# One more stage split of a four-layer graph network: joint row statistics, two relus moved to VectorE, a message summed in one PSUM bank, and new instruction orders

## The chip, the cores and the metric

The kernel runs on one core of a Trainium2 chip. The metric is the device time of one execution in microseconds (us), as the median of three runs.

## The reference

The input `x` has 128 graphs of 128 nodes with 256 features; `adj` is one 128 x 128 adjacency for all graphs. Four residual layers follow each other, each on `h = relu(layernorm(x))`:

```
layer 0: hW = h W0;  e = leaky(hW a_self + (hW a_neigh)^T);  x += [softmax(e + mask) hW, hW]      (W0: 256 -> 128)
layer 1: x += deg * (h Wi^T + b) + adj (h Wj^T)
layer 2: 8-head masked attention on h, projected by Wo, plus biases;  x += ...
layer 3: Wh = h W3;  e = leaky(Wh a_src + (Wh a_dst)^T);  x += softmax(e, masked) Wh
```

`layernorm` subtracts the row's mean and divides by `sqrt(var + 1e-5)`; it has no weights.

## The kernel before, in words

The 128 graphs are worked in 64 groups of two (`GROUP = 2`). Everything of one group is cut into some 130 pieces, each a small function such as `stats0_0`, `norm0_1`, `rows_hi0`, `move0`, `feat0`. The digit behind the name is the layer. Each engine runs its own list of pieces, `slot`, once per step `t`; `at(part, piece)` says that in step `t` the piece works on group `t - part`. So each engine works on up to eight groups in one step, and a step is what one group costs the engine in all. The order within `slot` was written out by a search, and engines are tied together by semaphores alone (`wait_ge(piece_done, g + 1)`).

```
        def run(slot):
            for t in range(graph_groups + PARTS):

                def at(part, piece):
                    if 0 <= t - part < graph_groups:
                        piece(t - part)
                slot(at)
```

A layer begins with the statistics on VectorE (`bn_stats` for each of the two graphs, L718 to L884, then `bn_aggr`), a few very small operations on GpSimd that make `rstd` and `nshift` of them (L1170 to L1264), and the relu on ScalarE (L964, L973, L1006, L1012, L1023, L1026, L1087, L1091), one instruction of 256 columns for each graph. GpSimd splits the result in two f16 halves (`rows_hi`, `rows_lo`, L1185 to L1272), SyncE turns them with a DMA transpose (`move0` to `move3`), and TensorE multiplies each product in three f16 passes (`triple`, L403 to L405). Results leave PSUM by ScalarE (hi halves, exps, leaky relus) and VectorE (lo halves, maxima, updates of `x`). In layer 2 the attention result of each graph is normalised in PSUM on VectorE (L850, L859), its hi half made on ScalarE (L1080, L1084) and its lo half on VectorE (L864, L868). In layer 1 the node's own message and the gathered one are summed in two banks and added to `x` by two VectorE instructions (`update1_own` L781, `update1` L786).

All eight PSUM banks have several users, one behind the other in a step, named in the table `f0_ps = ps[3]` and so on.

Of the kernel before, what the change touches and what calls it, by code (L numbers as in the profile page):

```python
# [12 lines left out]
P = 128  # L13
D = 256
# [7 lines left out]
FOLD = [0, 1, 2, 5]  # L22
# [4 lines left out]
UNSCALE = 1.0 / WEIGHT_SCALE  # L27
Q_SCALE = UNSCALE * float(DH) ** -0.5
# [4 lines left out]
PARTS = 7  # L33
# [9 lines left out]
def build(nc, x_in, adj, adj_t, w0, w0_t, a0, w_i, w_j, b1, w_q, w_k, b_qk, w_v, b_v, w_o, b_o, w3, w3_t, a3, out):  # L43
# [7 lines left out]
    with ctx:  # L51
# [15 lines left out]
        deg_unscale = sb("deg_unscale", [P, 1], F32)  # L67
# [26 lines left out]
        stats0 = pair("stats0", [P, GROUP, 6], F32)  # L94
        moments0 = pair("moments0", [P, GROUP, 2], F32)
        vareps0, rstd0, nmean0, nshift0 = (pair(n, [P, GROUP], F32) for n in ("vareps0", "rstd0", "nmean0", "nshift0"))
        relu0 = pair("relu0", [P, GROUP, D], F32)
        stats1 = pair("stats1", [P, GROUP, 6], F32)
        moments1 = pair("moments1", [P, GROUP, 2], F32)
        vareps1, rstd1, nmean1, nshift1 = (pair(n, [P, GROUP], F32) for n in ("vareps1", "rstd1", "nmean1", "nshift1"))  # L100
        relu1 = pair("relu1", [P, GROUP, D], F32)
# [1231 lines left out]
```

## Time and profile before

| what | value |
| --- | --- |
| three runs | 1141.29, 1141.49, 1145.17 us, median 1141.49 |
| span of the profiled execution | 1144.0 us |
| its own time | 1145.17 us (the only run that is not shorter than the span) |
| TensorE busy | 1054.0 us, 92% |
| VectorE busy | 1043.0 us, 91% |
| ScalarE busy | 1056.3 us, 92% |
| GpSimd busy | 949.6 us, 83% |
| mean granted TensorE clock | 0.987 of 2.4 GHz |

The span runs from the first to the last instruction of one execution. The busy shares are averages over the filling of the pipeline, the steady part and its draining. Most ScalarE and VectorE instructions start before the one ahead has ended, so what an instruction costs is the distance from its start to the next start, and not the duration printed for it.

### The profile page before, as it was taken

To read this page: it belongs to the slowest core of one execution; us is meant where nothing else is said; L and a number is where in the kernel's file an instruction comes from. 1 tells how busy PE (TensorE), PEld (TensorE's weight loads), DVE (VectorE), ACT (ScalarE), POOL (GpSimd) and SP (SyncE) were. 2 spreads that over 40 slices of the span, in tenths; PEclk is the share of its full clock that TensorE was granted. 3 is DMA by queue.
4 is the path that set the end of the run, shared out by engine and by line. 5 is a ranking of instruction groups with operands and counts; after the bars stand their busy time and mean duration, and the time that the engine had idled before them with its cause. 6 is when DMAs were issued, how large, how long until landed. Compare 5 with 4: busy or idle time off the path is not lost.

```text
span 1144.0 us, 38802 instructions
## 1 busy us (share of the span) xinstructions
PE 1054.0 (92%) x14872; PEld 883.0 (77%) x14872; DVE 1043.0 (91%) x2911; ACT 1056.3 (92%) x3145; POOL 949.6 (83%) x1734
## 2 busy tenths in 40 slices
PE   4689999999999999999999999999999999999964
PEld 3467888788878878887887888888888888888752
DVE  4489999999999999999999999999999999999961
ACT  3489999999999999999999999999999999999862
POOL 3888899889989989988898988889888988998521
PEclk9899999999999999999999999999999999999997
DMA  5369999999999999999999999999999999999872
GB/s 149 68 110 167 180 177 182 167 187 171 181 176 178 171 169 182 180 179 168 182 167 179 183 178 173 169 189 171 174 176 183 170 168 190 180 174 156 151 139 51
DMA packets 643514, 190.05 MB, mean 166 GB/s; under 512 B 607232, under 2 KB 643328, under 8 KB 643328
## 3 DMA queue, kind: packets, MB, share of 16 engines
q1 hardware_dynamic: 642560, 187.24, 94.9%
q8 instruction: 117, 1.92, 0.7%
q14 instruction: 69, 0.57, 0.2%
q10 hardware_dynamic: 768, 0.33, 0.1%
HBM read 19.73 MB, written 16.78 MB: 32 GB/s over the span
## 4 chain that ended last, share of the span: by engine, by line
ACT 47%; DMA 16%; POOL 14%; PE 12%; DVE 9%; issue 3%; POOLq 0%; SPq 0%; DVEq 0%
DMA h_t<-h_rows 11%; PE ps L403 3%; DMA mix_t<-mix_rows 3%; PE ps L405 3%; PE ps L404 3%; ACT ps L1053 3%; ACT ps L1042 3%; ACT ps L1048 3%; ACT ps L1059 3%; POOL h_rows L1189 3%; POOL h_rows L1249 2%; ACT relu L973 2%; ACT relu L964 2%; ACT query_hi L1030 2%; ACT key_hi L1033 2%
## 5 line engine op out<-in xcount | busy, mean ns | idle before, releaser
L403 PE MATMUL ps<-w_hi,h_t 128*128 128x256 f16 (+2 forms) x1280 | 330.5, 265 | 31.4 <-DMA h_t<-h_rows 28.3
L404 PE MATMUL ps<-w_lo,h_t 128*128 128x256 f16 (+2 forms) x1280 | 329.5, 264 | 0.0
L405 PE MATMUL ps<-w_hi,h_t 128*128 128x256 f16 (+2 forms) x1280 | 326.4, 264 | 0.0
L403 PEld LDWEIGHTS ps<-w_hi,h_t 128*128 128x128 f16 x1280 | 125.3, 98 | 53.7 <-DMA h_t<-h_rows 33.0
L403 PE MATMUL ps<-h_t,w_hi 128*128 128x256 f16 x512 | 139.6, 273 | 0.0
L405 PE MATMUL ps<-h_t,w_lo 128*128 128x256 f16 x512 | 139.6, 273 | 0.0
L404 PE MATMUL ps<-h_t,w_hi 128*128 128x256 f16 x512 | 139.6, 273 | 0.0
L405 PEld LDWEIGHTS ps<-w_hi,h_t 128*128 128x128 f16 x1280 | 125.6, 98 | 14.3
L404 PEld LDWEIGHTS ps<-w_lo,h_t 128*128 128x128 f16 x1280 | 126.3, 99 | 13.2
L1185 POOL TENSOR_SCALAR h_rows<-relu 128x512 f16<-128x512 f32 x64 | 39.5, 618 | 64.3 <-ACT relu L964 64.3
L403 PEld LDWEIGHTS ps<-v_hi,head_t_hi 128*128 128x128 f16 x1024 | 79.9, 96 | 8.8 <-issue 2.3
L404 PEld LDWEIGHTS ps<-v_lo,head_t_hi 128*128 128x128 f16 x1024 | 78.7, 96 | 6.9 <-issue 0.3
L403 PE MATMUL ps<-v_hi,head_t_hi 128*128 128x33 f16 x1024 | 84.0, 178 | 0.0
L405 PE MATMUL ps<-v_hi,head_t_lo 128*128 128x33 f16 x1024 | 83.9, 177 | 0.0
L404 PE MATMUL ps<-v_lo,head_t_hi 128*128 128x33 f16 x1024 | 83.9, 177 | 0.0
L1048 ACT ACTIVATE ps<-ps,head_nmax 128x128 f32<-128x128 f32 x256 | 82.6, 527 | 0.0
L1221 POOL TENSOR_TENSOR x<-x,deg_b 128x512 f32<-128x512 f32 x64 | 81.6, 1275 | 0.0
L1241 POOL TENSOR_TENSOR x<-x,out_bias 128x512 f32<-128x512 f32 x64 | 81.3, 1270 | 0.0
L1053 ACT ACTIVATE ps<-ps,head_nmax 128x128 f32<-128x128 f32 x256 | 79.8, 484 | 0.0
L405 PEld LDWEIGHTS ps<-v_hi,head_t_lo 128*128 128x128 f16 x1024 | 78.6, 96 | 0.0
L1189 POOL TENSOR_TENSOR h_rows<-relu,h_rows 128x512 f16<-128x512 f32 x64 | 74.0, 1156 | 5.4
L1216 POOL TENSOR_TENSOR h_rows<-relu,h_rows 128x512 f16<-128x512 f32 x64 | 74.0, 1156 | 5.3
(181 smaller groups left out, 4622.4 us busy)
## 6 DMA issues: line engine op xcount, KB each, us to landing
x<-in_x SPq DMA_DIRECT2D x64, 256.0 KB, 3.9
out<-x SPq DMA_DIRECT2D x64, 256.0 KB, 2.7
h_t<-h_rows SPq DMA_TRANSPOSE x256, 3.6
head_t_hi<-head_hi SPq DMA_TRANSPOSE x64, 4.7
head_t_lo<-head_lo SPq DMA_TRANSPOSE x64, 6.2
mix_t<-mix_rows SPq DMA_TRANSPOSE x64, 3.4
w_f<-in_w_o SPq DMA_DIRECT2D x1, 256.0 KB, 4.1
w3t_f<-in_w_t SPq DMA_DIRECT2D x1, 256.0 KB, 3.8
```

The costliest lines, as they stand in the source:

```text
L403: pe.matmul(o, lh, rh, start=start, stop=False)
L404: pe.matmul(o, lh, rl, start=False, stop=False)
L405: return pe.matmul(o, ll, rh, start=False, stop=stop)
L1042: last = act.activation(sc0_ps[:, j * P:(j + 1) * P], sc0_ps[:, j * P:(j + 1) * P], ACT.Exp, bias=head_nmax[g % 2][:, 0, j:j + 1])
L1048: last = act.activation(sc1_ps[:, j * P:(j + 1) * P], sc1_ps[:, j * P:(j + 1) * P], ACT.Exp, bias=head_nmax[g % 2][:, 1, j:j + 1])
L1053: last = act.activation(sc2_ps[:, j * P:(j + 1) * P], sc2_ps[:, j * P:(j + 1) * P], ACT.Exp, bias=head_nmax[g % 2][:, 2, j:j + 1])
L1059: last = act.activation(sc3_ps[:, j * P:(j + 1) * P], sc3_ps[:, j * P:(j + 1) * P], ACT.Exp, bias=head_nmax[g % 2][:, 3, j:j + 1])
L1185: pool.tensor_scalar(h0_rows[g % 2][:, 0, :, :], relu0[g % 2][:, :, :], 1.0, 0.0, ALU.mult, ALU.add).then_inc(rows_hi0_done, 1)
L1189: pool.tensor_tensor(h0_rows[g % 2][:, 1, :, :], relu0[g % 2][:, :, :], h0_rows[g % 2][:, 0, :, :], ALU.subtract).then_inc(rows_lo0_done, 1)
L1216: pool.tensor_tensor(h1_rows[g % 2][:, 1, :, :], relu1[g % 2][:, :, :], h1_rows[g % 2][:, 0, :, :], ALU.subtract).then_inc(relu_lo1_done, 1)
L1221: pool.tensor_tensor(x[g % XBUF][:, :, :], x[g % XBUF][:, :, :], deg_b1[:, :].unsqueeze(1).to_broadcast([P, GROUP, D]), ALU.add)
L1241: pool.tensor_tensor(x[g % XBUF][:, :, :], x[g % XBUF][:, :, :], out_bias[:, :].unsqueeze(1).to_broadcast([P, GROUP, D]), ALU.add)
```

## The change

The change has six parts.

1. **Joint statistics.** One `bn_stats` reads both graphs of a group, element by element in turn, so that its even and odd results are those of the two graphs. The eight `bn_aggr` and half of the eight `bn_stats` of a step go. `add_eps` and `shift` move from GpSimd to VectorE, `negate_mean` goes.
2. **Outer relus on VectorE.** For layers 0 and 3, `relu(x - mean)` is one `tensor_scalar` from SBUF to SBUF for each graph on VectorE; the division by the deviation is put off to the copy of the features out of PSUM on ScalarE (`scale=rstd`). `keep_feat0` becomes two instructions.
3. **Message summed in one bank.** `agg` carries the weight scale, `gather` adds into the bank of `message_own`, and one VectorE instruction updates `x`.
4. **Heads split on GpSimd.** VectorE writes the normalised heads to `mix_f` in SBUF; GpSimd makes both halves of it for both graphs at once.
5. **Query and key bias on 64-row halves.** The four bias matmuls of a step read 64 rows each, query from the lower and key from the upper half, and come ahead of both products.
6. **New orders.** `PARTS` is 9 and no longer 7, all six orders and the bank table are new.

```diff
-PARTS = 7
+PARTS = 9
...
-            def stats0_0(g):
-                dve.wait_ge(x_moved[g % XBUF], 32 * (g // XBUF) + 16)
-                dve.bn_stats(stats0[g % 2][:, 0, :], x[g % XBUF][:, 0, :]).then_inc(stats0_0_done, 1)
...
-            def mean_var0(g):
-                dve.wait_ge(stats0_0_done, g + 1)
-                dve.bn_aggr(moments0[g % 2][:, 0, :], stats0[g % 2][:, 0, :])
-                dve.bn_aggr(moments0[g % 2][:, 1, :], stats0[g % 2][:, 1, :]).then_inc(mean_var0_done, 1)
+            def both_stats0(g):
                 dve.wait_ge(x_moved[g % XBUF], 32 * (g // XBUF) + 16)
+                dve.bn_stats(stats0[g % 2][:, :, :].rearrange("p b s -> p (b s)"), x[g % XBUF][:, :, :].rearrange("p b d -> p d b")).then_inc(both_stats0_done, 1)
+
+            def add_eps0(g):
+                dve.tensor_scalar(vareps0[g % 2][:, :], stats0[g % 2][:, :, 2], DEFER_VAR, DEFER_EPS, ALU.mult, ALU.add).then_inc(add_eps0_done, 1)
...
+            def norm0_0(g):
+                dve.tensor_scalar(relu0[g % 2][:, 0, :], x[g % XBUF][:, 0, :], stats0[g % 2][:, 0, 1:2], 0.0, ALU.subtract, ALU.max).then_inc(norm0_0_done, 1)
...
+            def shift1(g):
+                dve.wait_ge(power1_done, g + 1)
+                dve.scalar_tensor_tensor(nshift1[g % 2][:, :], stats1[g % 2][:, :, 1], -1.0, rstd1[g % 2][:, :], ALU.mult, ALU.mult).then_inc(shift1_done, 1)
...
-            def update1_own(g):
-                dve.wait_ge(message_own_done, g + 1)
...
             def update1(g):
+                dve.wait_ge(add_deg_bias_done, g + 1)
                 dve.wait_ge(gather_done, g + 1)
...
+                dve.scalar_tensor_tensor(x[g % XBUF][:, :, :], mi_ps[:, :].rearrange("p (b n) -> p b n", b=GROUP), degree_unscale[:, 0:1], x[g % XBUF][:, :, :], ALU.mult, ALU.add).then_inc(update1_done, 1)
...
-            def norm0_0(g):
-                act.activation(relu0[g % 2][:, 0, :], x[g % XBUF][:, 0, :], ACT.Relu, bias=nshift0[g % 2][:, 0:1], scale=rstd0[g % 2][:, 0:1]).then_inc(norm0_0_done, 1)
...
+            def keep_feat0_0(g):
+                act.activation(g0[g % 2][:, 0, 1:1 + F0W], f0_ps[:, 0 * F0W:1 * F0W], ACT.Copy, scale=rstd0[g % 2][:, 0:1]).then_inc(keep_feat0_0_done, 1)
...
-            def keep_out_0(g):
-                act.wait_ge(head_norm_0_done, g + 1)
...
+            def rows_hi_mix(g):
+                pool.wait_ge(head_norm_0_done, g + 1)
+                pool.tensor_scalar(mix_rows[g % 2][:, 0, :, :], mix_f[g % 2][:, :, :], 1.0, 0.0, ALU.mult, ALU.add).then_inc(rows_hi_mix_done, 1)
+
+            def rows_lo_mix(g):
+                pool.wait_ge(rows_hi_mix_done, g + 1)
+                pool.tensor_tensor(mix_rows[g % 2][:, 1, :, :], mix_f[g % 2][:, :, :], mix_rows[g % 2][:, 0, :, :], ALU.subtract).then_inc(rows_lo_mix_done, 1)
...
+                for e in range(KC):
+                    for bank, row, first in ((q_ps, 0, e), (k_ps, P // 2, KC + e)):
+                        pe.matmul(bank[:, e * GROUP * P:(e + 1) * GROUP * P], qk_bias[row:row + P // 2, first * P:(first + 1) * P], unit_rows[row:row + P // 2, 0:GROUP * P],
+                                         start=(e == 0), stop=False)
```

In the new bank table, `p0_ps`, `s0_ps`, `mi_ps` and `q_ps` are all `ps[7]`.

The order of VectorE in the middle of a step, around the statistics of layers 0 and 2. Before:

```order
L792 BN_STATS stats_0<-x 128x6 [waits update1_done]
L795 BN_STATS stats_0<-x 128x6
L830 TENSOR_TENSOR head_lo<-ps,head_hi 128x512 [waits keep_head_0_done]
L723 BN_STATS stats_1<-x 128x6 [waits x_moved_4]
L718 BN_STATS stats_1<-x 128x6 [waits x_moved_4]
L799 BN_AGGR moments_0<-stats_0 128x2 [waits stats2_1_done]
L800 BN_AGGR moments_0<-stats_0 128x2
L727 BN_AGGR moments_1<-stats_1 128x2 [waits stats0_0_done]
L728 BN_AGGR moments_1<-stats_1 128x2
```

Now:

```order
L716 BN_STATS stats_0<-x 128x6 [waits x_moved_10]
L786 BN_STATS stats_0<-x 128x6 [waits update1_done]
L880 RECIPROCAL inv_1<-sum_1 128x2 [waits expo3_1_done]
L719 TENSOR_SCALAR vareps_1<-stats_1 128x2
L729 TENSOR_SCALAR relu_0<-x,stats_0 128x256 [waits both_stats0_done]
L836 TENSOR_TENSOR head_lo<-ps,head_hi 128x512 [waits keep_head_3_done]
L790 TENSOR_SCALAR vareps_0<-stats_0 128x2 [waits both_stats2_done]
L725 TENSOR_SCALAR relu_0<-x,stats_0 128x256
L865 TENSOR_SCALAR vareps_0<-stats_0 128x2
```

The two pairs of statistics have become two single ones. Three `add_eps` (L719, L790, L865) and both relus of layer 0 (L729, L725), which read and write SBUF, stand between the work on PSUM.

The order of GpSimd in the new kernel, from the addition of layer 1's bias on:

```order
L1155 TENSOR_TENSOR x<-x,deg_b 128x512
L1134 TENSOR_TENSOR rstd_1<-vareps_1,minus_half 128x2 [waits add_eps0_done]
L1196 TENSOR_SCALAR h_rows<-relu_1 128x512 [waits norm3_0_done]
L1150 TENSOR_TENSOR rstd_0<-vareps_0,minus_half 128x2 [waits add_eps1_done]
L1138 TENSOR_SCALAR h_rows<-relu_0 128x512 [waits norm0_0_done]
L1200 TENSOR_TENSOR h_rows<-relu_1,h_rows 128x512 [waits rows_hi3_done]
L1184 TENSOR_SCALAR mix_rows<-mix_f 128x512 [waits head_norm_0_done]
L1159 TENSOR_SCALAR h_rows<-relu_0 128x512 [waits norm1_0_done]
L1188 TENSOR_TENSOR mix_rows<-mix_f,mix_rows 128x512 [waits rows_hi_mix_done]
L1163 TENSOR_TENSOR h_rows<-relu_0,h_rows 128x512 [waits rows_hi1_done]
L1172 TENSOR_TENSOR x<-x,out_bias 128x512
L1192 TENSOR_TENSOR rstd_1<-vareps_1,minus_half 128x2 [waits add_eps3_done]
```

The small operations are gone but for the four powers (two of them, L1134 and L1150, and L1192 here); the split of the heads (L1184, L1188) has joined. GpSimd now waits for VectorE at `rows_hi3`, the powers and `rows_hi_mix`.

## Rows read from the trace of the kernel before

**Rows 1.** 160 to 960 us: busy PE, PEld, DVE, ACT, POOL; clock, DMA share, GB/s
```profile
160.00:960.00 800.00, 775.03 (x11215) 656.15 (x11214) 774.57 (x2176) 789.04 (x2368) 714.86 (x1306) 1.00 1.03 176
```

**Rows 2.** VectorE's L718 (all, then from 118.5 us) and L895: ns min/median/max, first and last start
```profile
L718 DVE BATCH_NORM_STATS2 stats<-x x64: 405/410/423, 4.5 to 1029.2; 128x6 f32<-128x256 f32 x64
L718 DVE BATCH_NORM_STATS2 stats<-x x56: 408/410/423, 118.6 to 1029.2; 128x6 f32<-128x256 f32 x56
L895 DVE SCALAR_TENSOR_TENSOR x<-ps,inv,x x64: 471/477/481, 113.3 to 1140.7; 128x256 f32<-128x256 f32 x64
```

**Rows 3.** The chain that ended last, one turn: start us, us, what
```profile
551.11 0.60 ACT query_hi L1030
...
559.41 4.82 DMA h_t<-h_rows
...
565.22 0.11 PE ps L523
...
567.87 0.60 ACT query_hi L1030
```

**Rows 4.** The same chain on ScalarE, whose pieces run from start to start
```profile
502.99 0.49 ACT relu L973
...
512.79 0.28 ACT mix_rows L1084
...
516.11 0.26 ACT leaky L988
```

**Rows 5.** Timeline of VectorE in one step: start us, us, engine, line, operation
```profile
544.74 0.64 DVE L786 TENSOR_TENSOR x<-ps,x 128x512 f32<-128x512 f32 x1
...
546.67 0.42 DVE L868 TENSOR_TENSOR mix_rows<-ps,mix_rows 128x256 f16<-128x256 f32 x1
...
547.34 0.42 DVE L792 BATCH_NORM_STATS2 stats<-x 128x6 f32<-128x256 f32 x1
547.67 0.41 DVE L795 BATCH_NORM_STATS2 stats<-x 128x6 f32<-128x256 f32 x1
...
549.43 0.17 DVE L799 BATCH_NORM_AGGREGATE moments<-stats 128x2 f32<-128x6 f32 x1
549.51 0.15 DVE L800 BATCH_NORM_AGGREGATE moments<-stats 128x2 f32<-128x6 f32 x1
```

**Rows 6.** GpSimd's groups from 160 to 960 us: count | busy us, mean ns | idle before
```profile
L1221 POOL TENSOR_TENSOR x<-x,deg_b 128x512 f32<-128x512 f32 x48 | 60.9, 1269 | 0.0
...
L1189 POOL TENSOR_TENSOR h_rows<-relu,h_rows 128x512 f16<-128x512 f32 x48 | 55.5, 1156 | 4.0
...
L1201 POOL TENSOR_TENSOR rstd<-vareps,minus_half 128x2 f32<-128x2 f32 x49 | 34.0, 693 | 0.0
...
L1212 POOL TENSOR_SCALAR h_rows<-relu 128x512 f16<-128x512 f32 x48 | 29.7, 619 | 0.1
...
L1197 POOL TENSOR_SCALAR vareps<-moments 128x2 f32<-128x2 f32 x49 | 9.4, 191 | 4.1
```

**Rows 7.** Timeline of the start: start us, us, engine, line, operation
```profile
8.68 1.16 POOL L1189 TENSOR_TENSOR h_rows<-relu,h_rows 128x512 f16<-128x512 f32 x1
...
9.50 0.62 DVE L683 TENSOR_SCALAR qk_bias<-qk_bias_f 128x512 f16<-128x512 f32 x1
...
11.87 0.43 DVE L698 TENSOR_SCALAR mask<-adj_f 128x512 bf16<-128x512 f32 x1
...
12.85 0.35 DVE L704 TENSOR_SCALAR deg_b<-b_row,degree 128x256 f32<-128x256 f32 x1
...
41.05 1.16 POOL L1216 TENSOR_TENSOR h_rows<-relu,h_rows 128x512 f16<-128x512 f32 x1
41.22 1.53 DVE L713 SCALAR_TENSOR_TENSOR w_lo<-w_f,w_hi 128x516 f16<-128x516 f32 x1
42.16 1.72 POOL L1221 TENSOR_TENSOR x<-x,deg_b 128x512 f32<-128x512 f32 x1
```

**Rows 8.** L713, all seven: ns min/median/max, first and last start
```profile
L713 DVE SCALAR_TENSOR_TENSOR w_lo<-w_f,w_hi x7: 657/676/1534, 14.5 to 41.2; 128x512 f16<-128x512 f32 x6, 128x516 f16<-128x516 f32 x1
```

More of the change, by code:

```diff
@@ L394, in _ @@
         def _(pe):
-            def turn(bank, src, b):
-                for c in range(KC):
-                    last = pe.transpose(bank[:, (c * GROUP + b) * P:(c * GROUP + b + 1) * P], src[:, b, c * P:(c + 1) * P], ident[:, :])
-                return last
             def triple(o, lh, ll, rh, rl, start, stop):
@@ L580, in project_0, with project_1 @@
                     pe.wait_ge(w_split, W_TURN.index("o") + 1)
+                for c in range(KC):
+                    last = triple(pr_ps[:, 0 * D:1 * D], mix_t[g % 2][:, 0 * KC + c, :], mix_t[g % 2][:, (GROUP + 0) * KC + c, :], w_hi[:, c, COL_WO:COL_WO + D], w_lo[:, c, COL_WO:COL_WO + D],
+                                  start=(c == 0), stop=(c == KC - 1))
+                last.then_inc(project_0_done, 1)
+            def project_1(g):
+                if g == 0:
+                    pe.wait_ge(w_split, W_TURN.index("o") + 1)
                 pe.wait_ge(move_out_done[g % 2], 16 * (g // 2) + 16)
@@ L683, in bias_rows @@
                     made(dve.tensor_scalar(rows, full, WEIGHT_SCALE, None, ALU.mult))
[L684 to L688 removed]
+                    for row in (DH, P // 2 + DH):
+                        last = dve.scalar_tensor_tensor(rows[row:row + 1, :], full[row:row + 1, :], WEIGHT_SCALE, rows[row:row + 1, :], ALU.mult, ALU.subtract)
+                    last.then_inc(bias_ready, 1)
                 dve.wait_ge(bqk_turned, 1)
@@ new lines, in slot @@
+                at(3, update0_1)
+                at(6, head_max_2)
+                at(3, both_stats1)
+                at(3, add_eps1)
+                at(4, split_message)
+                at(6, head_max_0)
+                at(7, invert_heads_1)
+                at(3, shift1)
+                at(7, head_norm_1)
+                at(7, invert_heads_0)
+                at(7, head_norm_0)
+                at(4, update1)
+                at(6, head_max_1)
+                at(0, both_stats0)
+                at(4, both_stats2)
@@ new lines, in slot @@
+                at(9, inv_sum3)
+                at(1, add_eps0)
+                at(0, norm0_1)
+                at(6, split_head_3)
+                at(4, add_eps2)
+                at(0, norm0_0)
+                at(8, add_eps3)
+                at(6, split_head_2)
+                at(6, split_head_0)
+                at(6, split_head_1)
+                at(2, row_max0)
+                at(5, split_query)
+                at(9, update3_1)
+                at(9, update3_0)
+                at(4, shift2)
```

643 lines of the change are left out of this document (267 added, 376 removed).

## The prediction

> **What bounds the kernel now.** I read the busy time of the steady part first, then the starts of two VectorE lines, then the chain of waits.
>
> From 160 to 960 us ScalarE is busy 789.04 of 800 us (98.6%), TensorE 775.03 (96.9%), VectorE 774.57 (96.8%), GpSimd 714.86 (89.4%) [rows 1]. The reader is to see that no engine has room: the four are within 10% of each other.
>
> L718 runs once a step. From its start at 118.6 to that at 1029.2 us lie 55 steps, so a step takes 910.6 / 55 = 16.56 us [rows 2]. Times the shares, a step has 16.33 us of ScalarE, 16.04 of TensorE, 16.03 of VectorE and 14.80 of GpSimd.
>
> The chain says how ScalarE's step is stretched at times: from one `query_hi` at 551.11 to the next at 567.87 us it goes once round, 16.76 us, over ScalarE's layer-0 relus, GpSimd, a transpose of 4.82 us and the key and query products [rows 3]. So it is ScalarE, and beside it a loop through ScalarE of the same length.
>
> The whole span splits into 4.5 us before the first L718, 114.1 us for the first 8 steps (14.3 each), 910.6 for the 55 full ones, 111.5 from the last L718 to the last L895 (7.7 steps of 14.5 by L895's place at the end of part 7), and 3.3 behind it: 1144.0 us [rows 2].
>
> **The change, part by part, in us per step.** Prices are distances between starts.
>
> ScalarE: four relus of 0.49 and two `mix_rows` of 0.28 go, 2.52 in all; the split `keep_feat0` adds at most one instruction like the 0.26 one of 128 columns [rows 4]. 16.33 becomes 14.07. ScalarE stops being the bound, and the loop above loses its relus. What this can give is limited by the engine that is next.
>
> VectorE, removed: eight statistics at 0.33 (547.34 to 547.67), 2.64; eight aggregates at 0.08 or slightly less, 0.60; `update1` at 0.56 (0.64 less the overlap of 0.08); two lo halves of the heads, 0.67 (546.67 to 547.34) [rows 5]. Sum 4.47.
>
> VectorE, added: four joint statistics of 512 columns. No row has one. Two of the old, 0.66, is the upper bound, the 0.56 of a 512-column instruction the lower [rows 5]; I take 0.60, since the old ones are slightly dearer than the tensor operations of their width, so 2.40. Four `add_eps` and two `shift` at the aggregate's 0.07 to 0.08: 0.44. Four relus: L704 has this form, 256 columns with a scalar for each row, and takes 0.35 [rows 7], 0.26 from start to start; 0.33 would be the old statistics' pace. I take 1.04. Two instructions (`add_eps1`, `head_norm_0`) now stand directly behind what they wait for, 0.09 each, the part of an instruction that a following one hides (0.17 against 0.08) [rows 5]: 0.17. Sum 4.05. VectorE falls by 0.42 to 15.6.
>
> TensorE: four bias matmuls of 0.11 [rows 3] become two pairs. If the two halves of the array run side by side 0.22 goes, if not nothing: 15.8 to 16.0. `gather` and `message_own` cost as before.
>
> GpSimd: twelve small operations of 0.19 go, two of 0.62 and 1.16 come [rows 6]: 14.80 - 2.28 + 1.78 = 14.3, or 14.5 since small ones overlap their neighbours.
>
> DMA: the same transposes and loads, 176 GB/s at a share of 1.03 [rows 1]. Transfers wait for GpSimd in a new order, with a step more between producer and consumer. I cost that at nothing; what covers it is the added depth. If the cover fails, `make_query` behind `move2` is late, as it is now.
>
> Depth: VectorE's pieces span parts 0 to 9. Ten steps fill the pipeline instead of eight, and from the last statistics of layer 0 to the last update are 9.4 steps instead of 7.7. If the latency of one group sets their length, both stay at 114 and 112 us; if each step keeps its length they become 143 and 136. I take the middle, 128 and 124, since the new steps hold fewer pieces each but the engines are 85% full there. So time = 4.5 + 128 + 124 + 3.3 + 53 P = 260 + 53 P for a steady step P. The old span is met at P = 16.68.
>
> **The shared path of VectorE and GpSimd.** This decides. In the steady part before, each VectorE instruction has an operand in PSUM, or is a statistic, aggregate, reduction or reciprocal; GpSimd's durations hardly vary. At the start other kinds meet it. L713, two operands in SBUF, takes 0.68 alone [rows 8]. The one at 41.22 takes 1.53: GpSimd's L1216 ran until 42.21, and L713 ended 0.54 behind that. GpSimd's next, L1221 at 42.16, took 1.72 instead of 1.27. L683, a `tensor_scalar` from SBUF to SBUF, took 0.62 where L698 of the same width took 0.43; GpSimd was busy until 9.84, and L683 ended 0.28 later [rows 7]. So these kinds of VectorE instruction wait for the GpSimd instruction in flight to end, but for the first 0.13 us (0.68 - 0.54), and GpSimd waits for them in turn.
>
> The new kernel puts four `tensor_scalar` relus and two `shift` with two SBUF operands into each VectorE step. GpSimd's new step has five instructions of 1.16, two of 1.27, five of 0.62 and five of about 0.70 [rows 6]. An arrival at a random time waits, on average, the sum of (T - 0.13) squared over twice the step: (5 x 1.03² + 2 x 1.14² + 5 x 0.49² + 5 x 0.57²) / (2 x 17.2) = 10.7 / 34.4 = 0.31 us. In the new order one of the six, `norm3_0`, comes when GpSimd itself waits for it (`rows_hi3`). Five pay: 1.55. Bounds are 0, if all fall into GpSimd's pauses, and 5 x 1.0, if each meets the start of a long one. I take the mean because nothing in the order keeps those places free.
>
> P = 15.6 + 1.55 = 17.15 and the span is 260 + 909 = 1169 us. The profiled execution's own time of 1145.17 us is 1.2 above its span and 3.7 above the median of the runs; so 1169 stands for a median of 1167 us, 2% slower.
>
> The Trainium skill, SBUF — State Buffer, section "Who interferes with whom", has this rule: `copy`, `cast` and `tensor_scalar` in a two-port mode, and instructions with two SBUF inputs, share one pair of ports with GpSimd, and who comes second blocks until the first is done. The rows at 9.50 and 41.22 us agree. The rule reaches further than the rows, to the 2-column `add_eps`; that is the second rival.
>
> **Rivals.**
>
> *A, faster: the meetings cost little.* GpSimd has to wait for VectorE at `rows_hi3`, at the powers and at `rows_hi_mix`. If the steps settle so that the relus run in these pauses, VectorE needs 15.6 to 15.8, TensorE 15.8 to 16.0. With 0.3 us of friction, less than the 0.5 that VectorE idles now (3.2% of 16.56), P = 16.1 and the time 260 + 853 = 1113, median 1111. For it: both relus of layer 0 stand near the `add_eps3` for which `power3` waits. Against it: GpSimd works 14.5 of 16 us. It decides up to 1.08 us of waiting per step (16.68 - 15.6); beyond that the change loses.
>
> *B, slower still: the `add_eps` block too.* Ten instructions of a step then need the shared path. Three meet a waiting GpSimd (`norm3_0`, `add_eps1`, `add_eps3`), seven pay 0.31, and `norm0_1` directly behind `add_eps0` finds the GpSimd instruction that slipped in between, 0.77 instead of 0.31 (the mean instruction of 0.9 less 0.13). P = 15.6 + 2.17 + 0.46 = 18.2 and the time 260 + 965 = 1225, median 1222. No row shows a 2-column case of VectorE. In the Trainium skill, VectorE: DVE Perf Modes, section "Mode 2×_2P", a `tensor_scalar` takes both ports when the outermost dimension is even, which 2 is; by that rule B and not my sum would hold.
>
> *C, no gain: bank 7.* `p0`, `s0`, `mi` and `q` follow each other in one bank within one step, over all three of TensorE, ScalarE and VectorE. If each is late by a place in its queue, the loop takes a step of 16.6 to 17 and the time is 1140 to 1161. Against it: 12 matmuls of 0.11 [rows 3] here and 12 there, with copies of half a microsecond, fill only some 10 us of a step.
>
> **How the numbers follow.** About 0.5% (5.7 us) is what a measurement of this kernel can tell from no change. The forecast has 0.47, of which 0.05 lies within 0.5%, where waits come near 1.08. A has 0.35, all faster. B has 0.12, all slower. C has 0.06, of which 0.05 is within 0.5%. So faster 0.35, same 0.10, slower 0.55. The range from 1090 to 1245 runs from A without friction (P = 15.8: 1097) and a somewhat shorter filling to B with the fill and drain at their upper bound; some 0.05 is left out below and 0.1 above. The forecast's own range is 1145 (waits of 1.1) to 1200 (2.2).
>
> **What would show it.** ScalarE's steady share falls from 98.6% to about 82%, VectorE's stays above 95%. `both_stats` takes about 0.68, the relus 0.35 when free and up to 1.4 otherwise, in step with the end of a GpSimd instruction; GpSimd's own durations spread. The distance of `both_stats0` starts gives P. A P below 16.5 with relus at 0.35 throughout shows the sum wrong; `add_eps` above 0.15 in most steps shows B. Fill and drain are read from the first ten and last nine starts.

## The result, and the profile after

The changed kernel takes 1255.82 us in the median of four runs (1254.50 to 1257.21), the kernel before on the same chip 1143.33. The ratio is 1.0987, 95% interval 1.0964 to 1.1009. The forecast was 1167 us with a range of 1090 to 1245. The direction was right; the size was not, and the time lies outside the range.

The steady part by windows, of the changed kernel (busy PE, PEld, DVE, ACT, POOL; clock, DMA share, GB/s):

```profile
160.00:960.00 800.00, 723.56 (x10037) 570.43 (x10036) 795.09 (x1736) 651.84 (x1909) 632.36 (x739) 1.00 0.91 158
```

Beside [rows 1]: VectorE went from 96.8% to 99.4% of the stretch, and everything else fell: TensorE to 90.4%, ScalarE to 81.5%, GpSimd to 79.0%. The granted clock is 1.00 in both, so it has no part in this step. The chain that ended last, by engine and by line, says the same:

```profile
DVE 85%; issue 5%; PE 4%; DMA 2%; ACT 2%; SPq 1%; POOL 0%; POOLq 0%; DVEq 0%
DVE relu L729 6%; DVE vareps L719 5%; DVE x L780 4%; DVE stats L862 3%; DVE stats L759 3%; DVE mj_lo L775 3%; DVE head_lo L821 3%; DVE stats L716 3%; DVE x L858 3%; DVE head_nmax L810 3%; DVE stats L786 3%; DVE head_nmax L832 3%; DVE head_nmax L817 3%; DVE relu L868 3%; DVE key_lo L802 3%
```

At its head stand a relu of 256 columns (L729, `norm0_1`) and an instruction of two columns (L719, `add_eps0`), ahead of all work on 512 columns. The starts of single lines (ns min/median/max, first and last start; L716 is `both_stats0`, all and from its eleventh start; L719 `add_eps0`, L729 `norm0_1`, L725 `norm0_0`, L868 `norm3_0`, L883 `update3_0`):

```profile
L716 DVE BATCH_NORM_STATS2 stats<-x x64: 686/699/707, 4.0 to 1118.2; 128x6 f32<-128x512 f32 x64
...
L716 DVE BATCH_NORM_STATS2 stats<-x x54: 693/699/702, 141.7 to 1118.2; 128x6 f32<-128x512 f32 x54
...
L719 DVE TENSOR_SCALAR vareps<-stats x64: 145/1105/1106, 12.8 to 1137.3; 128x2 f32<-128x2 f32 x64
L729 DVE TENSOR_SCALAR relu<-x,stats x64: 340/1435/1441, 4.8 to 1120.5; 128x256 f32<-128x256 f32 x64
L725 DVE TENSOR_SCALAR relu<-x,stats x64: 340/341/1237, 5.0 to 1122.5; 128x256 f32<-128x256 f32 x64
L868 DVE TENSOR_SCALAR relu<-x,stats x64: 336/677/752, 99.4 to 1234.3; 128x256 f32<-128x256 f32 x64
L883 DVE SCALAR_TENSOR_TENSOR x<-ps,inv,x x64: 466/468/477, 131.0 to 1249.6; 128x256 f32<-128x256 f32 x64
```

From 141.7 to 1118.2 us lie 53 steps: P = 976.5 / 53 = 18.42 us, where the forecast had 17.15. The span is 4.0 + 137.7 + 976.5 + 131.4 + 3.2 = 1252.8 us. The medians of L719 and L729 lie at their maxima: these two are late in nearly every step, and by the same amount. L725, the same instruction as L729 for the other graph, is not.

Timeline of VectorE and then of GpSimd over the same stretch of one steady step (start us, us, engine, line, operation):

```profile
598.42 0.29 DVE L765 TENSOR_SCALAR vareps<-stats,message_var,message_eps 128x2 f32<-128x2 f32 x1
598.62 0.74 DVE L775 SCALAR_TENSOR_TENSOR mj_lo<-ps,message_unscale,mj_hi 128x512 f16<-128x512 f32 x1
599.28 0.68 DVE L810 TENSOR_REDUCE head_nmax<-ps 128x4 f32<-128x512 f32 x1
...
603.49 0.15 DVE L880 RECIPROCAL inv<-sum 128x2 f32<-128x2 f32 x1
603.56 1.11 DVE L719 TENSOR_SCALAR vareps<-stats 128x2 f32<-128x2 f32 x1
604.58 1.44 DVE L729 TENSOR_SCALAR relu<-x,stats 128x256 f32<-128x256 f32 x1
605.93 0.68 DVE L836 TENSOR_TENSOR head_lo<-ps,head_hi 128x512 f16<-128x512 f32 x1
606.53 0.15 DVE L790 TENSOR_SCALAR vareps<-stats 128x2 f32<-128x2 f32 x1
606.60 0.34 DVE L725 TENSOR_SCALAR relu<-x,stats 128x256 f32<-128x256 f32 x1
606.86 0.15 DVE L865 TENSOR_SCALAR vareps<-stats 128x2 f32<-128x2 f32 x1
```

```profile
598.80 0.69 POOL L1150 TENSOR_TENSOR rstd<-vareps,minus_half 128x2 f32<-128x2 f32 x1 [0.99 <-DVE vareps L765]
...
602.36 1.16 POOL L1188 TENSOR_TENSOR mix_rows<-mix_f,mix_rows 128x512 f16<-128x512 f32 x1
603.48 1.16 POOL L1163 TENSOR_TENSOR h_rows<-relu,h_rows 128x512 f16<-128x512 f32 x1
604.59 1.27 POOL L1172 TENSOR_TENSOR x<-x,out_bias 128x512 f32<-128x512 f32 x1
607.10 0.70 POOL L1192 TENSOR_TENSOR rstd<-vareps,minus_half 128x2 f32<-128x2 f32 x1 [1.24 <-DVE vareps L865]
```

`add_eps0` starts 0.08 us after GpSimd's L1163 and ends at 604.67, 0.03 after L1163's end at 604.64. `norm0_1` starts 0.01 ahead of the start of L1172 and ends at 606.02, 0.16 after L1172's end at 605.86. From 605.86 to 607.10 GpSimd waits for `add_eps3` (L865), and all that VectorE does there on SBUF is free. So the two engines wait for each other in turn, both within 4 us. On the shared path itself only VectorE pays: GpSimd's instructions keep their length beside it (ns min/median/max from 160 to 960 us), though the forecast expected them to spread.

```profile
L1163 POOL TENSOR_TENSOR h_rows<-relu,h_rows x44: 1153/1156/1162, 161.3 to 953.6; 128x512 f16<-128x512 f32 x44
L1172 POOL TENSOR_TENSOR x<-x,out_bias x44: 1262/1268/1269, 162.4 to 954.7; 128x512 f32<-128x512 f32 x44
```

From start to start `add_eps0` takes 1.02 us where 0.07 is its free price (606.53 to 606.60 for L790), `norm0_1` 1.35 where 0.26 is (606.60 to 606.86 for L725). With `norm3_0` (mean 0.60) and `norm3_1` (0.38) the waits are 0.95 + 1.10 + 0.34 + 0.11 = 2.50 us per step. The other six of the ten pay nothing.

### The profile page after: what moved, and what is told of

It is laid out like the page before. It is cut to its first block, busy times and chain, and to the rows that moved or that the text cites. A ratio compares the mean times of both kernels' runs of the same rounds, so it can differ in the third digit from the quotient of the medians.

```text
span 1252.8 us, 37773 instructions
## 1 busy us (share of the span) xinstructions
PE 1089.4 (87%) x14872; PEld 855.1 (68%) x14872; DVE 1184.8 (95%) x2600; ACT 969.7 (77%) x2825; POOL 933.2 (74%) x1094
## 4 chain that ended last, share of the span: by engine, by line
DVE 85%; issue 5%; PE 4%; DMA 2%; ACT 2%; SPq 1%; POOL 0%; POOLq 0%; DVEq 0%
DVE relu L729 6%; DVE vareps L719 5%; DVE x L780 4%; DVE stats L862 3%; DVE stats L759 3%; DVE mj_lo L775 3%; DVE head_lo L821 3%; DVE stats L716 3%; DVE x L858 3%; DVE head_nmax L810 3%; DVE stats L786 3%; DVE head_nmax L832 3%; DVE head_nmax L817 3%; DVE relu L868 3%; DVE key_lo L802 3%
## 5 line engine op out<-in xcount | busy, mean ns | idle before, releaser
L978 ACT ACTIVATE prob<-leaky,nmax 128x128 f32<-128x128 f32 x64 | 25.8, 402 | 126.4 <-DVE nmax L735 126.4
L618 PE MATMUL ps<-g,prob_t 128*128 128x256 f32 x256 | 72.1, 405 | 31.9 <-DVE head_lo L836 31.0
L386 PE MATMUL ps<-v_hi,head_t_hi 128*128 128x33 f16 x1024 | 90.8, 178 | 9.8 <-DMA head_t_lo<-head_lo 3.5
L1150 POOL TENSOR_TENSOR rstd<-vareps,minus_half 128x2 f32<-128x2 f32 x64 | 44.9, 702 | 68.7 <-DVE vareps L765 68.7
L1192 POOL TENSOR_TENSOR rstd<-vareps,minus_half 128x2 f32<-128x2 f32 x64 | 44.9, 702 | 68.5 <-DVE vareps L865 68.5
L388 PE MATMUL ps<-v_hi,head_t_lo 128*128 128x33 f16 x1024 | 90.1, 177 | 0.0
L387 PE MATMUL ps<-v_lo,head_t_hi 128*128 128x33 f16 x1024 | 90.0, 178 | 0.0
L729 DVE TENSOR_SCALAR relu<-x,stats 128x256 f32<-128x256 f32 x64 | 85.6, 1337 | 0.0
L393 PE MATMUL ps<-ident,g 128*128 128x128 f32 x256 | 51.1, 282 | 39.2 <-DVE key_lo L802 31.4
L1155 POOL TENSOR_TENSOR x<-x,deg_b 128x512 f32<-128x512 f32 x64 | 84.2, 1315 | 0.0
L1172 POOL TENSOR_TENSOR x<-x,out_bias 128x512 f32<-128x512 f32 x64 | 81.2, 1269 | 0.0
```

The source lines that it names most:

```text
L386: pe.matmul(o, lh, rh, start=start, stop=False)
L387: pe.matmul(o, lh, rl, start=False, stop=False)
L388: return pe.matmul(o, ll, rh, start=False, stop=stop)
L393: pe.matmul(bank[:, b * P:(b + 1) * P], feats[:, b, col:col + 1].to_broadcast([P, P]), ident[:, :], start=(b == 0), stop=False, is_transpo ...
L618: last = pe.matmul(s3_ps[:, b * D:(b + 1) * D], prob_t3[g % 2][:, b * P:(b + 1) * P], g3[g % 2][:, b, 0:D], start=True, stop=True)
L729: dve.tensor_scalar(relu0[g % 2][:, 1, :], x[g % XBUF][:, 1, :], stats0[g % 2][:, 1, 1:2], 0.0, ALU.subtract, ALU.max)
```

## The experiments

Each kernel is compared with the kernel before on its own chip; steps are the mean distance of starts in the middle of the run, from the 21st start of layer 0's statistics to the 50th.

**1. The five moved behind row_max0.** The block L719, L729, L790, L725, L865 stands where GpSimd waits:

```diff
-                at(1, add_eps0)
-                at(0, norm0_1)
...
                 at(6, split_head_1)
                 at(2, row_max0)
+                at(1, add_eps0)
+                at(0, norm0_1)
+                at(4, add_eps2)
+                at(0, norm0_0)
+                at(8, add_eps3)
                 at(5, split_query)
```

> Edit: in VectorE's order of the changed kernel, add_eps0, norm0_1, add_eps2, norm0_0 and add_eps3 move as one block behind row_max0; nothing else. Theory S (waits on the path that VectorE shares with GpSimd): in the changed kernel add_eps0 and norm0_1 lose 0.95 and 1.10 us per step to the GpSimd instructions in flight; behind row_max0 GpSimd has finished add_out_bias and itself waits for add_eps3, so both run at 0.07 and 0.26 and the step falls from 18.42 to about 16.4 us, the span to 1115 to 1145. Rival L (VectorE's own load and the longer pipeline make the loss): the work is the same, so the step stays at 18.4 and the span at 1253.

1183.45 us, ratio 1.036 (1.0324 to 1.0396): 72 us come back without one instruction less. The step is 17.11. All five are free, but another waits now, `shift2` (L794); its line, and the place beside GpSimd's `add_feat0` (L1146):

```profile
L794 DVE SCALAR_TENSOR_TENSOR nshift<-stats,rstd x64: 160/623/637, 49.5 to 1120.1; 128x2 f32<-128x2 f32 x64
...
609.96 0.68 POOL L1146 TENSOR_TENSOR x<-x,g 128x256 f32<-128x256 f32 x1
610.03 0.63 DVE L794 SCALAR_TENSOR_TENSOR nshift<-stats,rstd 128x2 f32<-128x2 f32 x1
```

In the changed kernel it took 0.144 in the median. GpSimd finishes `power2`, for which `shift2` waits, and goes straight on to L1146; `shift2` comes 0.07 us too late. It costs 0.48 for the lock, and 0.2 more of the wait for `power2` ahead of it. So the step came to 17.11 and not 16.4.

**2. One column in place of two**, in `add_eps0` alone.

```diff
-                dve.tensor_scalar(vareps0[g % 2][:, :], stats0[g % 2][:, :, 2], DEFER_VAR, DEFER_EPS, ALU.mult, ALU.add).then_inc(add_eps0_done, 1)
+                dve.tensor_scalar(vareps0[g % 2][:, 0:1], stats0[g % 2][:, 0, 2:3], DEFER_VAR, DEFER_EPS, ALU.mult, ALU.add)
+                dve.tensor_scalar(vareps0[g % 2][:, 1:2], stats0[g % 2][:, 1, 2:3], DEFER_VAR, DEFER_EPS, ALU.mult, ALU.add).then_inc(add_eps0_done, 1)
```

> Edit: add_eps0 as two instructions of one column each instead of one of two columns, in the same place. Theory S with the rule that a tensor_scalar takes the shared ports only if its outermost dimension is even: both run at once, norm0_1 then meets the GpSimd instruction before (0.8 us) and add_eps2 the next one (0.4), so 2.05 becomes about 1.2 and the step about 17.6, the span about 1210. Theory S without that rule: one column blocks as well, step 18.4 or a little more. Rival L: 18.4 to 18.5, one small instruction more.

1214.67 us, ratio 1.0633 (1.0597 to 1.067), step 17.67. The first of the two single columns, in the run with them:

```profile
L719 DVE TENSOR_SCALAR vareps<-stats x64: 126/132/143, 12.7 to 1096.4; 128x1 f32<-128x1 f32 x64
...
602.15 1.16 POOL L1164 TENSOR_TENSOR h_rows<-relu,h_rows 128x512 f16<-128x512 f32 x1
...
602.34 1.12 DVE L730 TENSOR_SCALAR relu<-x,stats 128x256 f32<-128x256 f32 x1
```

In 64 cases the first never took over 0.143 us and the second (L720) never over 0.152, at the very place in the order where the two-column form took 1.105. The relu behind them (L730 here) now meets the same GpSimd instruction by itself and takes 1.12. So two columns take the shared path and one does not. In the Trainium skill, VectorE: DVE Perf Modes, section "Mode 2×_2P", the outermost dimension of more than one element must be even, or odd and equal on both sides, for `tensor_scalar` to use both ports; a single column has no such dimension, and both runs agree.

**3. The relus back on ScalarE**, the rest as changed. The bias is the negated mean, by one two-column reduction on VectorE for each layer:

```diff
-                dve.tensor_scalar(relu0[g % 2][:, 1, :], x[g % XBUF][:, 1, :], stats0[g % 2][:, 1, 1:2], 0.0, ALU.subtract, ALU.max)
+                dve.tensor_reduce(nmean0[g % 2][:, :], stats0[g % 2][:, :, 1:2], AX.X, ALU.max, negate=True).then_inc(negate_mean0_done, 1)
...
+                act.activation(relu0[g % 2][:, 1, :], x[g % XBUF][:, 1, :], ACT.Relu, bias=nmean0[g % 2][:, 1:2])
```

> Edit: the four outer relus of a step go back to ScalarE (relu of x minus the mean, still with the deviation put off), VectorE makes the negated means with one tensor_reduce per layer. Theory S: norm0_1 and norm3 lose 1.55 us of waits with 1.05 us of work; VectorE needs 15.0 plus up to 1.0 for add_eps0, ScalarE 15.0 + 1.96 = at most 17.0, so the step is 16.1 to 17.0 and the span 1130 to 1180. Rival L, with load alone: VectorE loses 1.05 us only, step 17.3, span about 1195.

1204.04 us, ratio 1.0538 (1.0502 to 1.0574), step 17.36: better, but a miss. The number is that of the rival, which counted VectorE's load alone (17.3), but the reason is another. `shift1`, `add_eps2` and `shift2`, all free in the changed kernel, wait here:

```profile
L768 DVE SCALAR_TENSOR_TENSOR nshift<-stats,rstd x64: 111/561/1115, 34.1 to 1112.0; 128x2 f32<-128x2 f32 x64
L789 DVE TENSOR_SCALAR vareps<-stats x64: 153/478/1119, 50.5 to 1132.4; 128x2 f32<-128x2 f32 x64
L793 DVE SCALAR_TENSOR_TENSOR nshift<-stats,rstd x64: 141/812/821, 51.4 to 1136.3; 128x2 f32<-128x2 f32 x64
```

Together these waits are 1.3 us per step, and VectorE idles 0.7 more for GpSimd's `power1`. Taking work away moves the meetings and does not end them.

**4. The kernel before with its outer relus on VectorE**, the rest as before, each pair directly behind its `mean_var`:

```diff
                 at(0, mean_var0)
+                at(0, norm0_1)
+                at(0, norm0_0)
...
                 at(6, mean_var3)
+                at(6, norm3_1)
+                at(6, norm3_0)
```

> Edit on the kernel before: the four outer relus alone move to VectorE (with the deviation put off to the copies of the features), behind the aggregates of their layer; seven parts, old order otherwise. Theory S: VectorE has 16.03 + 1.04 = 17.1 us of work and 0.3 to 0.6 us of waiting for each relu, 1.2 to 2.4 in all: step 18.3 to 19.5, span 1240 to 1305. Without a shared path: step 17.1, span about 1175. If the relus cost nothing where ScalarE is the bound: 1144 or less.

1194.83 us, ratio 1.048 (1.0429 to 1.0532), step 17.27. I had expected waits and there were none, a miss; the two relus of layer 3 on VectorE:

```profile
L897 DVE TENSOR_SCALAR relu<-x,moments x64: 352/353/355, 96.4 to 1171.5; 128x256 f32<-128x256 f32 x64
L900 DVE TENSOR_SCALAR relu<-x,moments x64: 345/348/350, 96.6 to 1171.8; 128x256 f32<-128x256 f32 x64
```

They stand directly behind the aggregate for which GpSimd's `add_eps3` waits. The relus of layer 0 are free too, 0.353 and 0.348 in the median. The loss here is VectorE's load alone: before, it was busy for 16.03 us of a step, and 4 x 0.265 more is 17.09; it is busy for 17.14 of 17.27. Moving these relus is wrong for this kernel even without the shared path.

**5. Joint statistics alone**, and **6.** with layer 3's relus on VectorE, and **8.** with both layers':

```diff
-                dve.bn_stats(stats0[g % 2][:, 0, :], x[g % XBUF][:, 0, :]).then_inc(stats0_0_done, 1)
...
+                dve.bn_stats(stats0[g % 2][:, :, :].rearrange("p b s -> p (b s)"), x[g % XBUF][:, :, :].rearrange("p b d -> p d b")).then_inc(mean_var0_done, 1)
```

> The kernel before with part 1 of the change alone: one joint bn_stats per layer, no bn_aggr; add_eps, negate_mean and shift stay on GpSimd, all relus on ScalarE. A joint statistic costs 0.60 to 0.62 us from start to start in the changed kernel, two old ones 0.66 and two aggregates 0.15, so VectorE loses 8 x 0.33 + 0.60 - 4 x 0.61 = 0.80 us of its 16.16 us of work per step. Theory L (each engine's own load): ScalarE keeps 16.36 us and stays the bound, so the step stays at 16.5 to 16.6 and the time between 1134 and 1143 us, ratio 0.993 to 1.0. Rival T (the four engines are tied so closely that any load taken from one shortens the step): step 16.2, about 1120 us.

1138.35 us, ratio 0.9964 (0.9947 to 0.9982), the only kernel of the study below the kernel before, and hardly. Its steady part:

```profile
160.00:960.00 800.00, 780.85 (x11298) 663.10 (x11287) 765.58 (x1612) 794.65 (x2391) 723.15 (x1315) 1.00 1.04 178
```

ScalarE is busy 99.3% where it was 98.6% [rows 1]: the bound was elsewhere. The instructions that went were dearer by 0.8 us than those that came, VectorE's busy time fell by 0.33 (16.03 to 15.70), and 0.15 of a step was bought.

> The kernel before with joint statistics and with the relus of layer 3 alone on VectorE (the deviation goes into the copy of the features; negate_mean3 and shift3 go from GpSimd). Theory L: ScalarE falls by two relus of 0.49 to 15.4 us, VectorE goes from 16.16 to 16.16 - 0.80 + 0.53 = 15.9, TensorE keeps 16.07. The step is then TensorE's and VectorE's, 16.1 to 16.3, and the time 1115 to 1130 us. Both relus stood at 0.27 from start to start, without a wait, when both layers were moved (0.262 and 0.269). Rival S (VectorE waits for GpSimd here too, now that the loads are closer): relus up to 0.6 each, step 16.6 and more, no gain over the kernel before.

1186.42 us, ratio 1.0379 (1.0356 to 1.0401): a clear miss. `norm3_1` is L854 here; its line, and its place beside `rows_lo0` (L1148):

```profile
L854 DVE TENSOR_SCALAR relu<-x,stats x64: 342/1169/1215, 90.3 to 1163.2; 128x256 f32<-128x256 f32 x64
...
607.38 1.22 DVE L854 TENSOR_SCALAR relu<-x,stats 128x256 f32<-128x256 f32 x1
```

```profile
607.28 1.16 POOL L1148 TENSOR_TENSOR h_rows<-relu,h_rows 128x512 f16<-128x512 f32 x1
```

The relu that was free in run 4 waits here 0.7 us on average and is late in nearly every step, since GpSimd is at L1148 when it comes. That this is so because layer 0's work stayed with ScalarE is likely, but no run shows it. These 0.7 us are most of the 0.9 by which the step of 17.15 missed the forecast's upper end.

> e4_before_relus_on_vector with joint statistics: the kernel before with both outer layers' relus on VectorE and no aggregates. That run had a step of 17.27 with VectorE never idle and no relu waiting, so VectorE's load alone set it. Theory L: 17.27 - 0.80 = 16.47, time 1191.3 - 53 x 0.80 = 1149 us, some 0.5% above the kernel before; more than with one layer moved. Rival S: with GpSimd's pauses (2.3 us per step there) shrinking, the relus begin to wait, step 17 and 1175 us.

1157.67 us, ratio 1.0142 (1.0119 to 1.0165), step 16.61. Two relus more on VectorE than in run 6, and 29 us less: here they are all free again (0.26 to 0.29 from start to start), as the sum of the loads said.

**7. The changed kernel with every wait mended.** The block of five stands as in run 1; beside it:

```diff
-                dve.scalar_tensor_tensor(nshift2[g % 2][:, :], stats2[g % 2][:, :, 1], -1.0, rstd2[g % 2][:, :], ALU.mult, ALU.mult).then_inc(shift2_done, 1)
+                dve.tensor_scalar(nshift2[g % 2][:, 0:1], stats2[g % 2][:, 0, 1:2], rstd2[g % 2][:, 0:1], -1.0, ALU.mult, ALU.mult)
+                dve.tensor_scalar(nshift2[g % 2][:, 1:2], stats2[g % 2][:, 1, 1:2], rstd2[g % 2][:, 1:2], -1.0, ALU.mult, ALU.mult).then_inc(shift2_done, 1)
...
-                at(8, norm3_0)
...
                 at(6, head_max_2)
+                at(8, norm3_1)
+                at(8, norm3_0)
                 at(3, both_stats1)
...
-                at(7, norm3_1)
...
+                at(4, power1)
                 at(9, rows_hi3)
-                at(4, power1)
```

> The changed kernel with the group of five moved behind row_max0 as in e1_group_later, and two places more mended: norm3_1 and norm3_0 stand directly ahead of both_stats1, with rows_hi3 on GpSimd behind power1, so that GpSimd waits for add_eps1 while they run; and shift2 is two one-column instructions with a pointer, which e2_one_column found free of the wait. Nothing of the computation is changed. e1_group_later had a step of 17.11, of which 0.48 was shift2's wait, 0.34 and 0.11 those of the norm3 pair. Theory S (the waits are the loss): step 17.11 - 0.93 + 0.10 = 16.28, first ten steps and drain as there (136, 130), span 7 + 266 + 53 x 16.28 = 1136 us. Rival M (GpSimd's lost time only comes up elsewhere): one of the other arrivals is blocked in its turn, or GpSimd becomes late, and the step stays above 16.8, over 1163 us.

1170.27 us, ratio 1.0238 (1.0213 to 1.0264): 85 us below the changed kernel. `norm0_1` (L729) and `norm3_0` (L869 here), and what VectorE waited for from 160 to 960 us (us in total, times, longest):

```profile
L729 DVE TENSOR_SCALAR relu<-x,stats x64: 339/346/1434, 4.7 to 1040.7; 128x256 f32<-128x256 f32 x64
L869 DVE TENSOR_SCALAR relu<-x,stats x64: 341/347/350, 98.0 to 1147.7; 128x256 f32<-128x256 f32 x64
...
DVE stats L716 <- DMA x<-in_x: 17.2, 24, 2.8
```

In the median all ten are free of the lock; single ones still meet it, `shift1` with up to 1.11 us. The shortest and commonest step is 16.41, 0.13 more than expected: with a column of SBUF as its scalar, each half of `shift2` costs 0.12 to 0.13 from start to start, where run 2 had shown 0.05 and 0.06 with constants. And the mean is 17.05, with single steps up to 19.3: a new wait, for the load of `x`, has come up. So the time is a miss too: a span of 1136 was expected and it is 1166, so that the rival's "over 1163" is met, though by a wait that it did not name.

**9. The load one step ahead**, on top of run 7:

```diff
-                at(0, load_x)
+                at(-1, load_x)
```

> e7_after_without_waits with load_x one step earlier in SyncE's order (a negative part, the buffer is free by then). In e7_after_without_waits most steps took 16.41 to 16.5 us but others up to 19.3, mean 17.05; VectorE waited 0.41 us per step, up to 2.8 at once, for the load of x, which SyncE issued only some 4 us ahead of both_stats0. Theory (late load): that wait goes, the mean step comes to 16.4 to 16.6 and the time to 4 + 133 + 126 + 3 + 53 x 16.5 = 1140 us, ratio 0.99 to 1.005. Rival (DMA and SyncE's queue are full, a load moved ahead makes the transposes late instead): step stays near 17.0, 1165 us.

1158.59 us, ratio 1.0141 (1.0119 to 1.0163). VectorE waits for no load any more, and the filling shortens (131 us). The commonest step stays 16.4, but a few long ones (17.9 to 19.4) remain, so the mean is 16.82 and the time 18 us above the expected 1140. Four of the long ones are those in which TensorE's granted clock falls to half, for 3.4 us each (from 251.7, 354.1, 589.6 and 958.2 us on). Here is the second, with the stretch ahead of it, in which TensorE waits 1.56 us for a transpose, and the one behind; then what VectorE waited for:

```profile
352.00:353.40 1.40, 0.00 (x0) 0.00 (x0) 1.40 (x3) 1.40 (x6) 1.40 (x2) 1.00 0.12 22
354.50:357.40 2.90, 2.90 (x16) 1.64 (x14) 2.26 (x6) 2.63 (x8) 2.90 (x3) 0.50 0.75 149
357.50:360.00 2.50, 2.50 (x25) 2.26 (x24) 0.55 (x1) 0.63 (x3) 0.20 (x1) 1.00 1.00 185
...
DVE nmax L735 <- ACT leaky L966: 6.5, 6, 2.0
```

At the lower level (1.2 GHz) 16 matmuls take 2.9 us, at the upper one (2.4 GHz) 25 take 2.5. Right behind it the leaky relus of layer 0 come late, and VectorE waits up to 2.0 us for them. These four steps hold some 9 us more than four of 16.5 (an estimate from their lengths). In the other profiled executions the clock falls only while the pipeline fills or drains. Why it falls here is not shown: in run 10 TensorE's weight loads wait up to 2.1 us for a transpose as well, and it does not fall.

**10. Layer 3's relus on ScalarE**, on top of run 9:

> e9_load_one_step_ahead with the relus of layer 3 back on ScalarE (bias is the negated mean, one reduction of two columns on VectorE). VectorE loses 2 x 0.26 and gains about 0.1 of its 16.3 us, ScalarE gains 2 x 0.49 to 16.0, TensorE has 16.1. If each engine's load sets the step now: 16.1 to 16.3, time 266 + 53 x 16.2 = 1125 us, ratio 0.98 to 0.99, ahead of both kernels. Rival: in e3_relus_on_scalar the relus on ScalarE came back as waits of shift1, shift2 and add_eps2 (1.3 us per step in all) because GpSimd no longer waited beside them; if so here, step 16.8 or more and 1155 us.

1161.41 us, ratio 1.0173 (1.0146 to 1.0199), step 16.7 nearly throughout, where 16.2 was expected. One wait of 0.6 in each step:

```profile
DVE head_lo L816 <- ACT head_hi L1029: 29.5, 48, 0.7
```

**11. keep_head_0 ahead of head_exp_1** on ScalarE, on top of run 10:

> e10_one_layer_on_scalar with keep_head_0 one place earlier on ScalarE, ahead of head_exp_1. There the step was 16.7 in nearly every case, with VectorE idle 0.61 us of it at split_head_0, which waits for keep_head_0, and ScalarE idle 0.61 at expo3_0. Theory (the step is set by this pair of queues): VectorE's wait goes, the step comes to 16.1 + some 0.2 of scattered waits = 16.3, the time to 4 + 129 + 130 + 3 + 53 x 16.3 = 1130 us, ratio 0.985 to 0.995, ahead of both kernels. Rival (the chain through the maxima and exps only closes elsewhere, ScalarE and VectorE wait in turns): step stays at 16.6 to 16.7, 1155 us.

1164.67 us, ratio 1.0199 (1.0167 to 1.0231), a miss: the same wait, one head further on.

```profile
DVE head_lo L823 <- ACT head_hi L1039: 29.7, 46, 0.7
```

**12. row_max3 ahead of both_stats3** on VectorE, on top of run 11:

> e11_keep_head_earlier with row_max3 ahead of both_stats3 on VectorE, for which ScalarE waited 0.6 us per step at expo3_0. Theory: where VectorE or TensorE's load sets the step this changes nothing (same as e11 within 0.5%); where ScalarE's chain does, 0.2 to 0.5 us per step less, 1105 to 1120 us. Rival: both_stats3 0.3 us later delays add_eps3 and power3, no gain or a loss of up to 0.5%.

1172.63 us, ratio 1.0257 (1.0228 to 1.0286): slower by more than allowed for; ScalarE now waits 0.5 us for the maximum of another head instead. So the step here seems to be set by the chain of maxima and exps between the two engines; that is read from the waits, as two swaps made by hand did not shorten it. Only run 5, the joint statistics alone, beats both kernels, the one before by 0.4%.

## Why the prediction was right and wrong

**The mechanism** stood as forecast: VectorE becomes the bound through waits on the path that it shares with GpSimd. Runs 1, 2 and 7 show it. With the waits on that path mended and the arithmetic unchanged, 85 of the 112 us that the change cost are gone; run 9, which moves the load too, brings it to 97. But the waits are no plain addend. Of 2.50 us, 1.45 came back: over the same 53 steps run 7 has a mean of 16.97, not 18.42 - 2.50 = 15.92 and still less the 15.6 of the forecast's sum. Its shortest step of 16.41 holds 0.18 for the split `shift2`, 0.18 of waiting for `power2` ahead of it and 0.12 at `inv_sum0` (L741, 0.08 to 0.20 from start to start); the rest of the mean are the late loads and single locks. So the first rival's P of 16.1 was not reached either, by this or any other run.

**The step that failed** is "An arrival at a random time waits, on average, ... 0.31 us", taken five times, 1.55 in all. The waits measured 2.50, and lie elsewhere: of the five that were to pay 0.31, `norm0_1` paid 1.10, `norm3_1` 0.11, and `norm0_0` and the two `shift` nothing. `norm3_0`, which was to be free because GpSimd would be waiting for it, paid 0.34, and `add_eps0`, which the sum left out, 0.95. Of the miss of 53 x (18.42 - 17.15) = 67 us, this is 53 x 0.95 = 50. Two things were wrong with it.

First, the number of arrivals. The two-column `add_eps` need the path as well, which was the second rival, and I gave it 0.12. It was right in kind, to the second half of its price: `norm0_1` behind `add_eps0` finds the next GpSimd instruction. Its step of 18.2 is 0.2 short of the measured one and its time of 1222 us 34 short, since it shares the sum of VectorE's work and the filling with the forecast. That its 2.63 us of waits come so near to 2.50 is partly luck: four of its seven payers paid nothing, and `norm3_0`, free by it, paid.

Second, the arrivals are not random. "Nothing in the order keeps those places free" was true, and nothing in it varies them either. Both engines start together once a step, at `add_eps1`, where GpSimd waits for VectorE, and then run without a pause. VectorE needs 5.14 us from there to `add_eps0` (598.42 to 603.56). GpSimd starts 0.38 later with the power, and comes to L1163 5.06 us after the same 598.42 (603.48). With the prices of before most of this sum could be made in advance: GpSimd's six instructions on the way are 0.69, 0.62 three times and 1.16 twice [rows 6], each some 0.04 less from start to start, and the next 1.16 is the one met. But the two starts lie 0.08 us apart, and `split_message` alone, on VectorE's way there, was priced 0.08 too low. So the prices could tell that `norm0_1` meets a long instruction, but not whether `add_eps0` is stopped as well: 2.05 us for the two, or about 1.25 for `norm0_1` and `add_eps2` as in run 2. The answer is a phase that holds for all steps: `add_eps0` always at the start of a 1.16, `norm0_1` always at the start of a 1.27. The results seen reach from 0 (runs 4 and, in most steps, 7) to 2.50, and the mean over them is no forecast. The forecast's own range, up to waits of 2.2, was too narrow for the same reason.

**The sum of VectorE's work** was 15.6, and measured 18.42 - 2.50 = 15.92. 0.12 of this is the joint statistics, 2.52 for four where I took 0.60 each: 0.61, 0.60 and 0.62, and 0.69 for `both_stats1`, whose result the next instruction needs. 0.08 is `split_message`, whose scalar is now a column of SBUF (0.66 from start to start, L775 at 598.62 to L810 at 599.28; the old form was not costed as changed). 0.11 is idle time in small gaps, the 0.6% of the step in which VectorE is not busy. Together 53 x 0.32 = 17 us.

**Filling and draining**: 137.7 and 131.4 where I took 128 and 124, 17 us of the miss. The upper bounds of 143 and 136 were nearer, as steps of 18.4 and not 17 go into them: in run 7, with a step of 17, the same stretches take 133.0 and 125.9. With the two sums above, 50 + 17 + 17 = 84 us is the whole distance from the forecast span of 1169 to the measured 1252.8.

**ScalarE, TensorE, GpSimd**: ScalarE's share fell to 81.5% (82 forecast), but of a longer step: 15.0 us, where the sum said 14.07. Start-to-start prices hold only while the next instruction covers the end of the one ahead; where ScalarE now pauses, the whole duration counts. `keep_head_1` takes 0.66 us before the next start where it took 0.53, `keep_head_2` 0.68 for 0.48, and so on, some 0.9 in all. It cost nothing, as ScalarE had room. GpSimd's busy time is 14.6 of a step; 14.5 was the forecast. The bias matmuls do run side by side; in the changed kernel all four stand in one group:

```profile
602.77 0.39 PE L489 MATMUL ps<-unit_rows,qk_bias 64*128 64x256 f16 x4
```

One lasts 0.27, and four in turn at 0.11 would be 0.27 + 0.33 = 0.60. This gain of 0.2 is worth nothing, for TensorE is not the bound. Bank 7, the third rival, does not appear in the chain, and with VectorE busy or blocked for 99.4% of the step it cannot be what sets it.

**Where the gain went.** The change takes six instructions and over 2 us of start-to-start time from ScalarE, the bound before, and some 0.2 from VectorE's busy time (16.03 to 18.31 - 2.50 = 15.81). Runs 4 and 8 show the first half of the answer: VectorE was busy for 16.03 us of a step of 16.6, so the four relus (1.05) need what the joint statistics give (0.80), and the step is 16.6 again with VectorE busy for 16.4 of it, with nothing gained (run 8). Without the locks the changed kernel's commonest step is 16.4 (run 7), hardly below the 16.6 before, and its mean is 16.97. Filling and draining do not cost the rest: the first ten steps and the time from the last statistics to the last update are 147.2 and 111.5 us before, 133.0 and 125.9 in run 7, the same in sum. It is 53 steps of 0.41 more, 22 us. The locks cost 85 us on top.

**Open**: why the clock falls in four steps of run 9, and whether a searched order could bring runs 10 to 12 to the 16.1 us that their loads would allow.

## What to carry to other kernels

Where two engines exclude each other for some instructions and run from one common wait, do not price a meeting by its mean: lay both queues side by side from that wait, with start-to-start durations, and see which instruction meets which. Where two starts come out closer together than the prices are exact, as the 0.08 us here, forecast both outcomes. A place that is free in one order is blocked in the next, so count every instruction that can take the shared path, the tiny ones too, and put them together where the other engine is waiting anyway. And before work is moved from a full engine, add it to the next: here that one was within 2% of the bound, and nothing was gained even where no relu waited (run 8).

## What had not been expected of the hardware

An instruction of two columns took 1.105 us in the median where it takes 0.15 when free, and the same work as two instructions of one column never took over 0.152 each. A two-column `scalar_tensor_tensor` with both operands in SBUF (L794 in run 1) is blocked as well (0.623). A blocked instruction is over at once when GpSimd's ends: 0.03 us later for two columns, 0.16 for 256. The order of the printed starts does not say who waits when they lie so close: `norm0_1` starts 0.01 us ahead of L1172 (604.58 and 604.59), and it is the one that is held. The Trainium skill, SBUF — State Buffer, section "Who interferes with whom", has the exclusion, and says that whoever issues first gets the ports; printed starts 0.01 us apart cannot settle that. That a blocked instruction can take seven times its free length, in nearly every step at the same place, is this case's to show.
